# Cross attention in a two-layer decoder: value scaling moved to GpSimd, key parts to SyncE's queue, and the scores' factor into the query weights

## What is computed

```python
q = (input @ Wq + bq).reshape(b, tq, H, D).transpose(0, 2, 1, 3)
kv = (encoded_features @ Wkv + bkv).reshape(b, tk, 2, H, D).transpose(2, 0, 3, 1, 4)
k, v = (kv[0], kv[1])
scores = jnp.einsum('bhqd,bhkd->bhqk', q, k) / math.sqrt(D)
attn = jax.nn.softmax(scores, axis=2)
out = jnp.einsum('bhqk,bhkd->bhqd', attn, v)
return out.transpose(0, 2, 1, 3).reshape(b, tq, H * D) @ Wo + bo
```

## Time and profile before

| | us |
| --- | --- |
| median of 3 runs | 1841.33 (1840.21 to 1843.25) |
| profiled execution | 1841.51 |
| its span in the trace | 1839.7 |
| full attention of layer 1, about | 723 to 1047 |
| cross attention, first key maximum to last update of x, about | 1047 to 1334 |

### The profile page before, as it was taken

The page is one execution under the profiler, slowest core; times in us unless marked ns, Lnnn a source line. Parts: engine busy times, 40 slices in busy tenths (PEclk is TensorE's granted clock), DMA queues, the critical chain, the costliest instruction groups (busy, mean ns, idle before and its releaser), DMA issues. The chain is left out here.

```text
span 1839.7 us, 32562 instructions
## 1 busy us (share of the span) xinstructions
PE 1548.8 (84%) x11264; PEld 1108.2 (60%) x11264; DVE 1225.7 (67%) x2066; ACT 929.6 (51%) x1746; POOL 624.7 (34%) x863
## 2 busy tenths in 40 slices
PE   4889986878999995688888878888644999999995
PEld 2445453568999994333333332232244999999995
DVE  3665552456788883777767467777767777777773
ACT  1344443133366662255645656757713666666662
POOL 5354430010155554634435423333011333333322
PEclk9899998989999997699999997987956999999998
DMA  5222220122288894421212312212043766767763
...
DMA packets 192834, 200.21 MB, mean 109 GB/s; under 512 B 33121, under 2 KB 167778, under 8 KB 192642
## 3 DMA queue, kind: packets, MB, share of 16 engines
...
## 5 line engine op out<-in xcount | busy, mean ns | idle before, releaser
L1713 PE MATMUL l1m_g_ps<-l1m_sb_rows_hi,l1m_sb_hi 128*128 128x256 f32 x736 | 210.1, 286 | 12.4 <-DVE l1m_sb_late L1612 11.0
L648 ACT ACTIVATE l1a_sb_probs<-l1a_s_ps,l1a_sb_kmax 128x512 f32<-128x512 f32 x256 | 172.7, 699 | 83.3 <-issue 55.4
L1713 PE MATMUL l1m_g_ps<-l1m_sb_rows_hi,l1m_sb_lo 128*128 128x256 f32 x736 | 209.6, 285 | 0.0
L1713 PE MATMUL l1m_g_ps<-l1m_sb_rows_lo,l1m_sb_hi 128*128 128x256 f32 x736 | 209.6, 285 | 0.0
L452 POOL DMA_DIRECT2D l1a_sb_kst<-l1a_sb_hi x256 | 125.6, 495 | 245.6 <-PE l1a_s_ps L768 213.1
L549 DVE TENSOR_REDUCE l1a_sb_mx<-l1a_s_ps 128x2 f32<-128x1024 f32 x128 | 154.0, 1218 | 62.3 <-PE l1a_s_ps L731 62.2
L583 DVE TENSOR_REDUCE l1a_sb_kmax<-l1a_s_ps 128x2 f32<-128x1024 f32 x128 | 153.1, 1217 | 41.4 <-PE l1a_s_ps L768 40.9
L654 ACT ACTIVATE l1a_sb_probs<-l1a_s_ps 128x1024 f32<-128x1024 f32 x128 | 128.0, 1022 | 88.5 <-PE l1a_s_ps L768 88.2
L549 DVE TENSOR_REDUCE l0a_sb_mx<-l0a_s_ps 128x2 f32<-128x256 f32 (+3 forms) x128 | 103.3, 820 | 80.4 <-PE l0a_s_ps L742 79.0
L768 PEld LDWEIGHTS l1a_s_ps<-l1a_sb_qst,l1a_sb_kst 49*128 49x128 f32 (+1 forms) x512 | 50.7, 199 | 174.2 <-issue 94.5
L768 PE MATMUL l1a_s_ps<-l1a_sb_qst,l1a_sb_kst 49*128 49x512 f32 (+1 forms) x512 | 131.6, 523 | 26.4 <-ACT l1a_sb_probs L648 21.5
...
## 6 DMA issues: line engine op xcount, KB each, us to landing
...
l1a_sb_qst<-l1a_sb_hi SPq DMA_DIRECT2D x256, 32.0 KB, 2.0
l1a_sb_kst<-l1a_sb_hi POOLq DMA_DIRECT2D x256, 32.0 KB, 2.0
l0a_sb_qst<-l0a_sb_hi SPq DMA_DIRECT2D x128, 32.0 KB, 2.1
l0a_sb_kst<-l0a_sb_hi POOLq DMA_DIRECT2D x128, 32.0 KB, 2.0
```

The lines of the kernel that those rows point to most:

```text
L648: ins = act.activation(probs[:, n % 8, e, :], at[:, e, :], ACT.Exp, bias=kmax[:, n % 4, e:e + 1], accum_out=zsum[:, n % 4, e:e + 1])
L1713: ins = pe.matmul(at, s, m, start=n == 0, stop=n == len(passes) - 1)
```

## The change

There are three parts to it, all for the cross batches.

1. **Values.** VectorE only inverts the sums, now into one of two buffers of `rzsum`, and waits for the scaling of two parts ago rather than one. GpSimd does the multiplication (its new `scale_v`).
2. **Keys' parts.** For batches 5, 6 and 7 SyncE issues the keys' 12 transfers of a stack right behind the queries' 12, with semaphores of their own (`kstacked_sp`); GpSimd's `stack` returns at once there. Batch 4 stays as it was.
3. **Factor.** At the layer norm of batch 2 GpSimd multiplies the queries' weights (128x512) and biases (128x2) by SCALE in place. The queries are then split like the keys, with two readings of `m_ps`, and the bank is handed back at `lo`. TensorE and VectorE wait once for this (`q_scaled`).

```diff
@@ -269,7 +269,7 @@
         mT = sb("mT", [GH, NG, T], F32R)
         kmax = sb("kmax", [P, 4, 2])
         zsum = sb("zsum", [P, 4, 2])
-        rzsum = sb("rzsum", [P, 2, 2])
+        rzsum = sb("rzsum", [P, 2, 2, 2])
         nothing = sb("nothing", [P, 1])
         one_row = sb("one_row", [1, T], F32R)
 
...
@@ -325,8 +328,6 @@
                 return m_act, b, use if use < 2 else use - 4
             if causal:
                 return m_dve, b, use - 2
-            if kinds[b] == "cross" and use % 2 == 0:
-                return m_dve, b, use // 2 - 1
             return lo_done, b, use - 2
 
 
...
@@ -354,11 +355,23 @@
 
         STACKED = 6 * 16
 
+        def by_sp(b):
+            return b > 0 and kinds[b - 1] == "cross"
+
+        def kstack_in(eng, b, p):
+            if by_sp(b):
+                eng.wait_ge(kstacked_sp[p], (b - B) * STACKED)
+            else:
+                eng.wait_ge(kstacked[p], (b + 1) * STACKED)
+
         def stacks_wait(eng, b, i):
 
             if b:
                 for p in range(4 * (i // 2), 4 * (i // 2) + 4):
-                    eng.wait_ge((kstacked if i % 2 else stacked)[p], b * STACKED)
+                    if i % 2:
+                        kstack_in(eng, b - 1, p)
+                    else:
+                        eng.wait_ge(stacked[p], b * STACKED)
 
         def in_part(parts, i, p, e):
             at = 32 * (p % 4) + 16 * e
...
@@ -398,6 +411,14 @@
                     for e in range(2):
                         for n, source in enumerate((hi, lo, hi)):
                             sp.dma_start(in_stack(qst, p, e, n), in_part(source, i, p, e)).then_inc(stacked[p], 16)
+                if by_sp(b):
+                    hi_done.wait(sp, b, i + 1)
+                    lo_done.wait(sp, b, i + 1)
+                    for p in (2 * g, 2 * g + 1):
+                        for e in range(2):
+                            for n, source in enumerate((hi, hi, lo)):
+                                sp.dma_start(in_stack(kst, p, e, n), in_part(source, i + 1, p, e)
+                                             ).then_inc(kstacked_sp[p], 16)
 
             def rows(b, g, _):
 
...
@@ -431,6 +452,12 @@
                                    ).then_inc(ln_rstd.sem, 1)
                 if b == 1 and has_cross:
                     pool.memset(vscaled[:, :, :, :], 0.0).then_inc(zeroed, 1)
+                if b == 2 and has_cross:
+
+                    w = parts[1]
+                    pool.wait_ge(w["in"], 5 * 16)
+                    for at in (w["wqkv"][:, :, 0:D], w["bqk"][:, 0:CC]):
+                        pool.tensor_scalar(at, at, SCALE, None, ALU.mult).then_inc(q_scaled, 1)
 
             def bias(b, *_):
 
...
@@ -442,6 +469,8 @@
                                    ).then_inc(x_biased.sem, 1)
 
             def stack(b, g, _):
+                if by_sp(b):
+                    return
                 i = 2 * (g // 2) + 1
                 hi_done.wait(pool, b, i)
                 lo_done.wait(pool, b, i)
...
@@ -465,7 +494,22 @@
                                    .unsqueeze(1).to_broadcast([P, NT, GH, HD]), ALU.add
                                    ).then_inc(v_biased.sem, 1)
 
-            run({"LN1": ln, "LN2": bias, "STACK": stack, "V": v_group})
+            def scale_v(b, g, kt):
+                if kinds[b] != "cross":
+                    return
+                m_act.wait(pool, b, 3)
+                if b % B == 0 and g == 0 and kt == 0:
+                    pool.wait_ge(zeroed, 3)
+                w = NT * g + kt
+                rz_done.wait(pool, b, w)
+                pv_done.wait(pool, b - 1, w)
+                at = HD * (g % 2)
+                pool.tensor_tensor(vscaled[:, kt, GH * g:GH * g + GH, at:at + HD],
+                                   v[:, b % 2, kt, GH * HD * g:GH * HD * (g + 1)].rearrange("p (h d) -> p h d", d=HD),
+                                   rzsum[:, w % 2, :, :].rearrange("p n e -> p (n e)").unsqueeze(2).to_broadcast([P, GH, HD]),
+                                   ALU.mult).then_inc(v_scaled.sem, 1)
+
+            run({"LN1": ln, "LN2": bias, "STACK": stack, "V": v_group, "W": scale_v})
 
         @block.vector
         def _(dve):
...
@@ -514,19 +560,10 @@
                                              ).then_inc(m_dve.sem, 1)
                     return
                 stacks_wait(dve, b, i)
-                if kinds[b] == "cross" and i % 2 == 0:
-                    lo_done.wait(dve, b, i - 1)
-                    dve.tensor_scalar(qk[:, 0, :], src, bias, SCALE, ALU.add, ALU.mult).then_inc(m_dve.sem, 1)
-                    m_dve.wait(dve, b, i // 2)
-                    dve.tensor_copy(hi[:, i, :], qk[:, 0, :]).then_inc(hi_done.sem, 1)
-                    hi_done.wait(dve, b, i)
-                    ins = dve.tensor_tensor(lo[:, i, :], qk[:, 0, :], hi[:, i, :].bitcast(F32), ALU.subtract)
-                else:
-                    dve.tensor_scalar(hi[:, i, :], src, bias, None, ALU.add).then_inc(hi_done.sem, 1)
-                    hi_done.wait(dve, b, i)
-                    ins = dve.scalar_tensor_tensor(lo[:, i, :], src, bias, hi[:, i, :].bitcast(F32), ALU.add,
-                                                   ALU.subtract)
-                ins.then_inc(lo_done.sem, 1)
+                dve.tensor_scalar(hi[:, i, :], src, bias, None, ALU.add).then_inc(hi_done.sem, 1)
+                hi_done.wait(dve, b, i)
+                dve.scalar_tensor_tensor(lo[:, i, :], src, bias, hi[:, i, :].bitcast(F32), ALU.add, ALU.subtract
+                                         ).then_inc(lo_done.sem, 1)
 
             def rest(b, use, _):
                 if not causal:
...
@@ -583,27 +620,15 @@
                 dve.tensor_reduce(kmax[:, n % 4, :], buffer("S", b, g, j)[:, :, :], AX.X, ALU.max, negate=True
                                   ).then_inc(kmax_done.sem, 1)
 
-            def scale_v(b, g, kt):
+            def inverse_sums(b, g, kt):
                 if kinds[b] != "cross":
                     return
-                m_act.wait(dve, b, 3)
-                if b % B == 0 and g == 0 and kt == 0:
-
-                    dve.wait_ge(zeroed, 3)
                 w, n = NT * g + kt, 8 * g + 2 * kt
                 exp_done.wait(dve, b, n + 1)
-                v_scaled.wait(dve, b, w - 1)
-                dve.reciprocal(rzsum[:, :, :], zsum[:, n % 4:n % 4 + 2, :]).then_inc(rz_done.sem, 1)
-                rz_done.wait(dve, b, w)
-
-                pv_done.wait(dve, b - 1, w)
-                at = HD * (g % 2)
-                dve.tensor_tensor(vscaled[:, kt, GH * g:GH * g + GH, at:at + HD],
-                                  v[:, b % 2, kt, GH * HD * g:GH * HD * (g + 1)].rearrange("p (h d) -> p h d", d=HD),
-                                  rzsum[:, :, :].rearrange("p n e -> p (n e)").unsqueeze(2).to_broadcast([P, GH, HD]),
-                                  ALU.mult).then_inc(v_scaled.sem, 1)
-
-            run({"LN1": ln, "LN2": normal, "PREP": prep, "LO": rest, "OUT": out, "S": key_max, "W": scale_v,
+                v_scaled.wait(dve, b, w - 2)
+                dve.reciprocal(rzsum[:, w % 2, :, :], zsum[:, n % 4:n % 4 + 2, :]).then_inc(rz_done.sem, 1)
+
+            run({"LN1": ln, "LN2": normal, "PREP": prep, "LO": rest, "OUT": out, "S": key_max, "W": inverse_sums,
                  "A": row_max, "Z": invert})
 
         @block.scalar
...
@@ -700,6 +725,8 @@
                     i = use - 2
                     if b % B == 0 and i == 0:
                         pe.wait_ge(w["in"], 5 * 16)
+                        if cross:
+                            pe.wait_ge(q_scaled, 2)
                     m_act.wait(pe, b, 1)
                     if cross and i == 1:
                         pe.wait_ge(ctx_in, (b % B + 1) * 16)
```

More of the change, by code:

```diff
@@ L285, in attention @@
         kstacked = [sem(f"kstacked{p}") for p in range(NPAIR)]
+        kstacked_sp = [sem(f"kstacked_sp{p}") for p in range(NPAIR)] if has_cross else None
+        q_scaled = sem("q_scaled")
         row_in = [sem(f"row_in{g}") for g in range(NG)]
@@ L505, in prep @@
                     dve.wait_ge(part(b)["in"], 5 * 16)
+                    if kinds[b] == "cross":
+                        dve.wait_ge(q_scaled, 2)
                 i, src = use - 2, product(b, use)
```

6 lines of the change are left out of this document (3 added, 3 removed).

## The result

The changed kernel takes 1835.43 us in the median of 6 runs (1832.36 to 1839.36), the kernel before 1842.29 (6 runs). The ratio is 0.9967 with a 95% interval of 0.9954 to 0.998, which is 3.7 to 8.5 us less. The forecast was 1835.4: faster, and inside its range.

A forecast was written before the change was run, and what follows sets the result against it. No engine is full, so the bound was read slot by slot, such as ScalarE in slot 3, TensorE in slot 1. Gains of 6.1 us less 0.2 made 5.9 off 1841.5: 1835.6, or 1835.4 against the median; range 1827 to 1841.

The forecast's parts named there:

- the two waits around the projection: Slot 0, queries' first half: TensorE's projection waits for `lo`, its next product for the update of x; 0.5 us saved.
- the split in slot 1: Slot 1: the half of the queries ahead of the `lo` that TensorE waits for; 0.4 us saved.
- The update of x: Slot 0: VectorE's update of x comes 0.5 us earlier; if it came later, the forecast would be wrong.
- D: Rival: the bank held 0.75 us longer for each of 8 queries' halves is the path; 6.0 us slower, 1847.3, chance 0.08.
- Scaling the weights once: Full attention: two GpSimd instructions, 1.3 + 0.2 us, cost 0; at worst all 1.5 us delay one stack.
- Batch 3 splits batch 4's queries and scales nothing: 0.5: Batch 3, which splits batch 4's queries the new way and scales no values: a gain of 0.5 us.
- One scaling (0.2): Slot 1: one values' scaling stands ahead of the `lo` TensorE waits for, 0.2 us saved; the others save 0.
- Slot 3, held at 10.5 us: Slot 3: ScalarE's exponentials cover all four scalings, so the gain is 0 and the slot stays at 10.5 us.
- B: Rival: VectorE sets the pace everywhere, so all 16.0 us come out: 1825.3; chance 0.12 including what lies between.
- What GpSimd saves is worth 0: Keys' parts leaving GpSimd for SyncE: the time GpSimd saves gains 0, as it was busy 9.7 of 25.3 us at most.
- a cover of 3.9 us: Values on GpSimd: TensorE needs a part three steps after its inversion, 3.9 us at the fastest pace.
- Keys on SyncE: cost 0: SyncE's queue in batches 5 to 7: a stack's issue grows from 7.6 to 15.2 us, the queue holds, cost 0.

The follow-up runs named there:

- SyncE's queue (0.9993): The kernel before with keys' parts on SyncE, and GpSimd's addition of the bias to x held until VectorE's first scaling of the slot: 1840.78 us, ratio 0.9993.
- all fourteen kernels: The kernel before, the changed kernel, and the follow-up kernels with single parts, parts undone or further edits: medians from 1815.45 to 1854.9 us.

## Why the prediction was right, and where its steps failed

**Right:** the time, and these steps as they stand in the profile: parts of 0.29 us (0.33), TensorE waiting for them only at the end, the projection's wait of 1.30 us, slot 2 of batch 5 shorter by 0.4 us at nearly the same clock (0.3), no wait for SyncE's transfers, the two waits around the projection 0.5 us less together (0.5), the split in slot 1, 0.5 us (0.4). The transposes of slot 0 start 6.7 us behind its start and not 6.9 (I had 0.4 less). The update of x is 0.8 us earlier in batch 6 (19.7 us behind the slot's start, 20.5 before) and 1.0 later in batch 5, where the low clock lies on other instructions; so this sign, which was to tell D, tells nothing by one trace. By the letter it came up for D in batch 5; the waits tell it apart.

**The full attention, at 0 or a gain, was a loss.** "Scaling the weights once" stood at 0, since GpSimd has idle time there. I asked when GpSimd is idle and not who runs beside it: VectorE's normalization does, takes 1.65 us and not 1.37, and TensorE waits 0.3 us longer. And "Batch 3 splits batch 4's queries and scales nothing: 0.5" had the sign of the second half wrong. There the transposes of the maxima want the bank next, and the second reading of it costs 0.8 us: theory D, in a batch whose rows the prediction had not read, since it took the cross attention's alone. With the low clock behind these waits the changed kernel's full attention is 5.8 us longer in its profile, and the cross attention 8.9 us shorter, not 5.9 (8.7 by the windows above).

**Slot 1 mis-sized.** "One scaling (0.2) [...] the other scalings lie beside TensorE's products: 0." The values alone took 1.1 us off it: four parts of 0.27 us, all on the path. That VectorE falls behind TensorE over the whole slot, and that the 0.97 us wait for `lo` is only where it shows, is my reading. With the split the slot is 17.8 us in batches 4 to 6, where it was 19.3, 19.8 and 19.6: some 5 us, where I had 1.8. These slots are at or near full clock before and after, and this is the largest part of the gain. The part itself, 0.27 and not 0.20, belongs to this too.

**Slot 3, held at 10.5 us, shortens.** At full clock it is 10.1 us in the changed kernel. By the prediction's own sign this speaks for B: VectorE was on the path there too, for 0.4 us a slot. It is not B as priced, since all 16 us did not come out. Why ScalarE's pace did not hold it at 10.5 is not shown.

**"What GpSimd saves is worth 0: it was busy 9.7 of 25.3 us at most" is false.** I took the busy share, and took each edit by itself. With the values on GpSimd, what counts is how long its queue is blocked at a stretch: twelve issues, some 7 us, against a cover of 3.9 us, which I had worked out and never held against a stack. Keys back on GpSimd cost 17 us.

**"Keys on SyncE: cost 0" is true of SyncE's queue (0.9993) and false of the edit by itself (1.0048).** I asked who waits for the parts, not what GpSimd does in the time it gets. The Trainium skill's page SBUF — State Buffer, section Who interferes with whom, says that a VectorE `tensor_tensor` with both inputs in SBUF contends with a GpSimd instruction that reads SBUF, that the lock on the ports they share is exclusive, and that the order of issue decides who blocks. By that rule the scaling ends once the addition, which began first, is over; the trace agrees, 1134.29 against 1134.21. In the changed kernel VectorE has no such instruction at that place, so the price never comes.

So the three parts are not terms of a sum. Alone they are 7, 6 and 9 us slower than before; together 6 us faster. Values and keys hold each other's cost: the keys must go for the values to be on time, and the values must go for the addition to be harmless.

**The clock.** I had it as a reason for the width. It is more: alone the parts run at 0.913 to 0.915, the whole at 0.920, which by the line among runs of one kernel is 5 us or so. Which idle stretch meets which busy one is not open to a walk through the trace of before. That 5.9 came out was partly luck: slot 1's gain was too small by some 3 us, and what the split cost in the full attention was not in the sum.

**Open:** what sets where the low-clock stretches fall, and why the last stage, with the same instructions in all fourteen kernels, takes 506.2 to 513.5 us in their profiles at a clock of 0.90 or 0.91. Up to 7 us of the difference between two profiles can be that.
